# TensorE's order in a windowed attention: one step at a time, or two steps together

## The reference, cut to what matters

```python
scores = jnp.einsum('bhqd,bhkd->bhqk', q, k) / jnp.sqrt(jnp.float32(DH))
allowed = (diff >= 0) & (diff < WIN)
scores = jnp.where(allowed, scores, -jnp.inf)
attn = jax.nn.softmax(scores, axis=-1)
ao = jnp.einsum('bhqk,bhkd->bhqd', attn, v)
...
x1 = x + g * attn_out + (1.0 - g) * ssm_out
h2 = _layernorm(x1, ln2_g, ln2_b)
mlp = jax.nn.gelu(h2 @ W1 + b1, approximate=False) @ W2 + b2
return x1 + mlp
```

## Time and profile before

| | |
|---|---|
| runs of the kernel before | 5219.56, 5221.64, 5172.90 us (median 5219.56) |
| profiled execution | 5248.13 us, span 5246.3 us |
| granted TensorE clock, mean | 0.928 of full speed |
| TensorE busy over the span | 82% |
| VectorE, ScalarE, GpSimd busy | 57%, 47%, 44% |
| layer-1 attention phase | about 2750 to 4860 us of the span |

### The profile page before, as it was taken

The page is one execution under the profiler, slowest core; times in us unless marked ns, Lnnn a source line. Parts: engine busy times, 40 slices in busy tenths (PEclk is TensorE's granted clock), DMA queues, the critical chain, the costliest instruction groups (busy, mean ns, idle before and its releaser), DMA issues. The chain is left out here.

```text
span 5246.3 us, 152203 instructions
## 1 busy us (share of the span) xinstructions
PE 4322.6 (82%) x61044; PEld 3367.0 (64%) x61140; DVE 2994.6 (57%) x7226; ACT 2465.0 (47%) x5553; POOL 2300.0 (44%) x2391
## 2 busy tenths in 40 slices
PE   3888898888888868888858988888888888888556
PEld 3776776676677757777746666566666656666555
DVE  3777777777767657777654344444444444443444
ACT  3554545554544423323325455555555555555334
POOL 4666666666656400000004444444444444443443
PEclk8999999999999989999979799899999989999579
DMA  2212212222221110000010000000000000000332
GB/s 82 52 44 62 64 47 56 65 49 53 63 56 44 42 51 17 24 24 16 24 60 9 1 8 8 8 8 8 8 8 8 8 8 8 8 8 5 120 96 91
DMA packets 151975, 186.91 MB, mean 36 GB/s; under 512 B 28254, under 2 KB 112353, under 8 KB 149985
## 3 DMA queue, kind: packets, MB, share of 16 engines
q1 hardware_dynamic: 144528, 160.98, 11.4%
q0 software_dynamic: 6864, 17.99, 0.9%
HBM read 68.48 MB, written 44.19 MB: 21 GB/s over the span
## 5 line engine op out<-in xcount | busy, mean ns | idle before, releaser
L1571 POOL TENSOR_TENSOR c_prob<-c_prob,c_inv 128x512 f32<-128x512 f32 (+1 forms) x512 | 484.1, 952 | 825.8 <-DVE c_inv L1824 807.5
L1654 ACT ACTIVATE c_prob<-c_s_ps,c_nmax 128x256 f32<-128x256 f32 (+1 forms) x1024 | 454.2, 453 | 312.0 <-DVE c_nmax L1819 304.9
L1819 DVE TENSOR_REDUCE c_nmax<-c_s_ps 128x2 f32<-128x512 f32 (+1 forms) x512 | 317.4, 620 | 404.8 <-PE c_s_ps L2021 401.6
L848 POOL TENSOR_TENSOR a_swap<-a_swap,a_sin 128x512 f32<-128x512 f32 x128 | 203.0, 1586 | 563.0 <-DMA a_swap<-a_raw 563.0
L2033 PE MATMUL c_t_ps<-c_ident,c_prob 128*128 128x128 f32 x1792 | 321.6, 298 | 14.3 <-POOL c_prob L1571 12.7
L889 ACT COPY a_raw<-a_w_ps 128x512 f32<-128x512 f32 x256 | 150.3, 587 | 350.4 <-PE a_w_ps L74 350.0
L212 POOL TENSOR_TENSOR b_var<-b_mv,b_eps 128x4 f32<-128x4 f32 x16 | 8.5, 533 | 695.4 <-DVE b_mv L304 695.3
L1665 ACT COPY c_pT<-c_t_ps 128x512 f32<-128x512 f32 (+1 forms) x512 | 276.7, 540 | 56.9 <-PE c_ab_ps L2051 55.0
L1170 PE MATMUL a_w_ps<-a_mem,a_sT 64*32 64x65 f32 x14848 | 216.2, 226 | 100.3 <-issue 96.8
L2021 PE MATMUL c_s_ps<-c_k,c_q 64*128 64x256 f32 (+1 forms) x1024 | 257.8, 333 | 22.8 <-issue 20.1
L1170 PEld LDWEIGHTS a_w_ps<-a_mem,a_sT 64*32 64x32 f32 x14848 | 170.2, 106 | 152.1 <-issue 131.1
(11 more groups left out here) (377 smaller groups left out, 13836.9 us busy)
## 6 DMA issues: line engine op xcount, KB each, us to landing
a_swap<-a_raw SPq DMA_DIRECT2D x1024, 64.0 KB, 2.1
d_xb<-sorted_rows SPq DMA_DIRECT2D x71, 130.0 KB
a_x_ln<-x SPq DMA_DIRECT2D x128, 64.0 KB, 2.1
a_acc<-x SPq DMA_DIRECT2D x64, 128.0 KB, 2.8
after_attn<-a_acc SPq DMA_DIRECT2D x64, 128.0 KB, 2.4
b_x_in<-after_attn SPq DMA_DIRECT2D x16, 512.0 KB, 4.4
after_ffn<-b_acc SPq DMA_DIRECT2D x16, 512.0 KB, 3.2
c_x_in<-after_ffn SPq DMA_DIRECT2D x16, 512.0 KB, 4.2
```

What stands on the lines that cost most here:

```text
L848: nc.gpsimd.tensor_tensor(q_sw, q_sw, table(sin), ALU.mult)
L1571: nc.gpsimd.tensor_tensor(p, p, inv[:, n % 4].unsqueeze(2).to_broadcast([P, 2, KB])[:, :, keys_of(i)], ALU.mult).then_inc(norm_ready, 1)
L1654: last = nc.scalar.activation(prob[:, n % 4, h, keys_of(i)], s_ps[:, n % 2, h, keys_of(i)], ACT.Exp, bias=nmax[:, n % 4, h:h + 1], accum_o ...
L1819: nc.vector.tensor_reduce(nmax[:, n % 4], s_ps[:, n % 2, :, keys_of(i)], AX.X, ALU.max, negate=True).then_inc(max_ready, 1)
```

## The change

Only TensorE's program in `attn1_phase` is changed; no instruction is added or taken out, and the other engines' programs stay as they are. TensorE now takes the steps in pairs (n, n + 1) for even n: both spreads, both scores, both transposes, both value products. The lags stay 3 and 5, so the pair (n, n + 1) has `scores` of n and n + 1, `transposes` of n - 3 and n - 2, `values` of n - 5 and n - 4. `mix` stays behind iterations 17, 25 and 33; the second group of the next input's transposes moves from behind iteration 30 to behind iteration 31.

```diff
-                for n in range(NS + LAG_P):
-                    if n + 2 < PAIRS1:
-                        spread_qk(it, n + 2)
-                    if n < NS:
-                        scores(it, n)
-                    if LAG_T <= n < NS + LAG_T:
-                        transposes(it, n - LAG_T)
-                    if n >= LAG_P:
-                        values(it, n - LAG_P)
-                    if n in (17, 25, 33):
-                        mix(it, (n - 17) // 8)
-                    if n in (27, 30) and not last_step(it):
-                        h_transposes(it + 1, (n - 27) // 3)
+                for n in range(0, NS + LAG_P + 1, 2):
+                    pair = (n, n + 1)
+                    for k in pair:
+                        if k + 2 < PAIRS1:
+                            spread_qk(it, k + 2)
+                    for k in pair:
+                        if k < NS:
+                            scores(it, k)
+                    for k in pair:
+                        if LAG_T <= k < NS + LAG_T:
+                            transposes(it, k - LAG_T)
+                    for k in pair:
+                        if LAG_P <= k < NS + LAG_P:
+                            values(it, k - LAG_P)
+                    if n in (16, 24, 32):
+                        mix(it, (n - 16) // 8)
+                    if n in (26, 30) and not last_step(it):
+                        h_transposes(it + 1, (n - 26) // 4)
```

## The result

| | before | changed |
|---|---|---|
| median of the runs | 5197.77 us (5172.9 to 5221.64, 4 runs) | 5422.33 us (5410.46 to 5437.16, 4 runs) |
| span of the profiled execution | 5246.3 us | 5418.0 us |
| granted TensorE clock, mean | 0.928 | 0.888 |

The ratio is 1.0434, 95% interval 1.0363 to 1.0505: the change makes the kernel 225 us slower. I had predicted 5295 us, slower by 75. The sign was right and the size three times too small: the measured time lies 2 us above the end of my range. (The kernel before has a fourth run here, so its median is 5197.77 and no longer the 5219.56 us that I had added the +75 to.)

The account below looks back on a forecast made before the run. TensorE was taken to set the pace, 3.80 us for two steps. First steps +5.3, paired steps +1.6, end -1.5 gave +5.4 us a sequence, +86 in 16; less 12 for the clock, about +75 on 5219.56: 5295 us, range 5195 to 5420.

Parts of the forecast that it names:

- Value products in pairs, transposes in pairs: On TensorE, two steps' value products cost about 0.60 us instead of 1.14, two transpose groups about 1.05 instead of 1.16.
- TensorE's own 3.15 us for a pair: TensorE's work for two steps without waits: scores 1.50, transposes 1.05, value products 0.60, instead of 3.80 us.
- the ring: Paired steps: value products, pT copy, exp, second scores, transposes wait in a circle; 4.10 us a pair, 3.80 before.
- my term -0.65: Passages with a mix between pairs: ScalarE is hidden and TensorE's own time counts, 3.15 instead of 3.80 us.
- my term +0.78: Passage where ScalarE's copy of the mix also stands in the circle of waits: +0.48 us on top of +0.30.
- six plain passages: Six of ten pair-to-pair passages between iterations 10 and 30, without a mix or its copy: +0.30 us each, +1.8 together.
- The first steps at full clock: Spread 2 to value products 5: spreads wait for copies; about 24.5 us instead of 19.2, a loss of 5.3 a sequence.
- The end: Value products 25 to 31, the end of a sequence: 7.9 us instead of 9.4, a gain of 1.5.
- the clock's term: Half-clock stretches stay in 3 sequences; four pairs in each gain 0.7 us instead of losing 0.3: -12 us in all.
- the clock falls in more sequences: Rival, chance 0.20: stretched first steps bring more falls, up to 13.7 us each; all 13 give 5470 us, a third 5350.
- my half-clock sum: Paired steps at half clock: the circle of waits takes 5.9 us a pair against 6.62 before, a gain of 0.7.
- my main case: Whole kernel: the paired steps' circle of waits with the clock as before, 5260 to 5330 us, chance 0.50.

Follow-up runs that it names:

- filled kernel: Changed kernel plus unneeded filler matmuls on TensorE in the first steps and in front of the pairs' second scores; 5333.98 us, ratio 1.0211.

## Why the prediction was right and where it failed

- **Value products in pairs, transposes in pairs:** right, 0.66 and 1.03 us for two. TensorE's own 3.15 us for a pair came out as 3.13 when the ring was taken away (V13 to V15, in all 16 sequences).
- **The ring:** right to 0.02 us at full clock, and its place too. With a mix between the pairs the passage takes 5.24 us (before 5.92, so -0.68; my term -0.65), with the copy of a mix in the ring 4.57 (+0.76; my term +0.78). At half clock it takes 5.91 us where the kernel before takes 6.63; my sum had 5.9 and 6.62. Taking the pT copies from between the exps removed it.
- **What bounds the kernel before:** right for single steps, but not for all. "TensorE sets the pace, 3.80 us for two" holds where VectorE has nothing else to do; V9 to V11 takes 4.25 us and V17 to V19 4.60, against 3.81 in the last sequence. My six plain passages at +0.30 each were really +0.80, +0.95, -0.16, +1.01, -0.51 and +0.27 (filled kernel against before). That they add up to +2.4, near my +1.8, is luck in part.
- **The first steps at full clock:** predicted 24.5 us from spread 2 to V5, measured 24.6 in the filled kernel. The marks on the way fit too: spread 2 to spread 4 took 5.30 against 5.22, transposes(5) came at 20.2 against 20.1, V3 at 21.2 against 21.05.
- **The end:** V25 to V31 is 8.25 us against 9.41, a gain of 1.2 where I had 1.5.
- **The sum at full clock:** +5.4 predicted, +6.3 measured in the filled kernel; the difference lies in the middle (45.44 instead of 43.39 us from V5 to V25, +2.05 where I had +1.6), up to 0.5 us of it the fillers' own, and in the end. It makes 14 us in the whole kernel.
- **The clock:** this step failed. In my sum the clock's term was -12 us, for falls as before; measured it is +107 (16 x 6.7). I gave "the clock falls in more sequences" a chance of 0.20 and wrote against it that "about the same thin stretch passed without a fall in 13 sequences". It fell in all 16, in the first steps in every one. It was not the same stretch: the change stretched it from 19.2 to 24.6 us with hardly more work in it, by the numbers of my own paragraph on the first steps, and it lengthened the waits in the pairs. Behind V9 the clock fell a second time in each sequence, each time right behind a wait of 1.38 us (the copy of a mix in the ring) or of 1.64 to 1.79 (VectorE's normalisation besides); the plain pair's 0.90 us that I had forecast brought it down nowhere by itself. VectorE's part in these waits is not in my prediction at all. The 3 sequences of 16 that fell before were evidence that the stretch stood at the edge and would fall when thinned; I read the other 13 as evidence of safety. Where all fall, my rival gave 5470 us, and my range left that case out by its own words. Of my signs for being wrong the last one came true: the clock row changed by more than a few stretches.
- **The size of a fall:** I put it at 13.7 us for each further sequence. In the kernel before, two of the three falls have 31 us at half clock and the third 61 us, in a sequence of 153.8 us from first spread to first spread. The falls cost the changed kernel 9.7 us in a sequence for about 37 us at half clock, less than in rows 1, as my half-clock sum had it: at half clock the ring's wait is covered by TensorE's slower work. With the clock's 16 x 6.7 = 107 us my sum would have been 5.4 x 16 + 107 = 193 us and the forecast 5413 us, where 225 us and 5422 were measured. That these come so close is luck in part, as the 225 us are against another median than my 5219.56. The likeliest number should have been near the end of my range, and the end further out.
- **The base:** my main case took the clock as it was, three falls at their old places. That case, with a chance of 0.50, had no ground in the rows: it assumed that the clock takes a stretch 5.3 us longer as it took the old one.

The Trainium skill, TensorEngine Tiling (Array Packing), section PSUM Bottleneck, says that the copy out of PSUM may become the bottleneck of a tiled TensorE. By its busy share ScalarE was not (2.78 us of work in a pair of 4.08); it was the place of the copy in the order. The same skill, TensorE: Matmul & The Clock Gate, section A second HAM failure mode: psum-queue depth-cycling, says that short idle times of TensorE between groups of matmuls can make the clock swing. The traces agree: no wait of the changed kernel's scores was above 2.0 us, and the clock fell in every sequence, in the ring right behind waits of 1.38 to 1.79 us. I had drawn on another section of that page and not on this one.

## What to carry to other kernels

When work is grouped on one engine, the engine that feeds it must be reordered in the same groups: a copy that waits for the end of a group and stands in front of what the next group needs makes a ring, and its length could here be summed from the timeline beforehand to 0.02 us. Look also at what the other engines do beside the group: VectorE's side work, 3.19 us in one piece, made the longest waits here. Before trusting such a sum, look where in the kernel TensorE's clock falls now, even if rarely: here a stretch where it fell in 3 of 16 sequences was one where it fell in all of them once the stretch got thinner, and where a change to another engine's program alone brought it down in seven, 1 per cent slower. A few useless matmuls in that stretch are the test, and here also a cure: they took the falls away and cost 1 us a sequence in the kernel before.

## What was not expected of the hardware

- Sixteen value products at four column quarters last 0.66 us, as long as eight do; the second step of a pair is free on TensorE in every pair, not in the last group only.
- The clock fell from 2.4 to 1.2 GHz behind idle pieces of 1.2 to 1.8 us between small matmuls, and in the first steps of the kernel before, whose matmuls are few and small, with no idle piece above 0.8 us. In the changed kernel it cost a net 6.7 us in each sequence, where one takes 133 us before.
- Adding work to the slow place made kernels faster: from 1.0434 to 1.0265 of before in the change, from 1.0103 to 0.9916 in the kernel before with VectorE's work spread.
- A kernel that is faster at full clock can be slower as a whole: 21.66 instead of 22.46 us in a stage, and 1.0103 of the time.
- A loop body of TensorE with 55 more matmuls for each sequence in it cost about 2.4 us before the first spread, with no wait that the profile names ([2.56 <-issue]), while an instruction queue moved 125 packets instead of 11; the cause was not tested.
